# Causal masks of an attention kernel: from TensorE mask matmuls to VectorE, on one Trainium2 core

## Chip, cores and metric

The kernel runs on one core of a Trainium2 chip (trn2). The metric is the device time of one launch in microseconds (us). TensorE is called PE below, its weight loads PEld, VectorE DVE, ScalarE ACT, GpSimd POOL, and the DMA-issuing SyncE SP.

## What is computed

The input is x of shape (4, 1024, 256), 16 heads of size 64. Cut to what matters here:

```
q, k, v = x @ Wq, x @ Wk, x @ Wv                      # per head, (1024, 64)
scores  = where(causal, q @ k.T / 8, -inf)            # 1024 x 1024, lower triangle
attn    = softmax(scores)
y       = x + concat(attn @ v) @ Wo ; layernorm, gamma, beta
x       = layernorm(x + y)
x       = layernorm(x + (silu(x @ wg.T) * (x @ wu.T)) @ wd.T)
```

The softmax subtracts each row's maximum, so each score is needed twice: once for the maximum over its row, and once, with the maximum subtracted, for the exponential.

## The kernel before

The work is 4 batches times 4 groups of four heads ("quads"), so 16 iterations; each has 4 heads x 9 = 36 steps, 576 steps in all (`g`), at an average of about 2.4 us. Every engine has its own program, a loop over `g` (lines 763, 900 and the like) whose order was written out by hand; semaphores join them.

Only blocks of the lower triangle are computed. For the exponentials, scores lie with keys on the partitions and queries along the free axis, in 9 banks of 512 columns per head (`PIECES`, line 36 on); five of the nine, `k` = 0, 2, 5, 7, 8 (`DIAG`), hold one or two 128 x 128 blocks that the diagonal crosses. For the maxima, scores are computed a second time, in one pass and with queries on the partitions, in 9 banks per head (`MAXB`), 13 steps ahead (`MAX_LEAD`); five of these hold diagonal blocks (`MDIAG`): banks 0, 2, 3, 4, 6. Since 13 = 9 + 4, a step with a `DIAG` bank always carries an `MDIAG` bank, so of nine steps five have both masks and four have none.

One step `g` on PE (`step`, line 727): `scores(g)` (line 623; K1 with Q1 then K2 with Q2, two matmuls a piece, L637), in one step of nine a transpose of the maxima (L621), `max_bank` (L607), then the masks: `scores_mask(g)` (L645) and `max_mask` (L614). Each is a bf16 matmul of an identity with a 128- or 256-column mask tile that adds -1e30 in PSUM. Then `pv(g-2)` (L664), the probabilities times V in three terms. After that come "fillers" in fixed steps of the iteration: projections (L531), V (L556), the output projection (`wo_unit`, L592), and, from iteration 5 on, the feed-forward tail (`t_transpose` L687, `t_up` L710, `t_down` L722). Steps 7 to 9 and 22 to 31 of an iteration have few or no fillers.

The others, in step `g`:

- ACT: copies out of finished banks, then `exp(g)` (line 809): waits for `st_mm` (the scores bank with its mask), L813 writes the probabilities in fp32, L816 writes them again, rounded (`probs_hi`, semaphore `hi_done`).
- POOL: `probs_lo(g)` (L1114), the difference of the two; PE's `pv(g)` waits for it (`lo_done`). POOL also does the norm of the heads (L1120), the low part of the feed-forward (`t_hl`, L1156) and small statistics.
- DVE: `step` (line 1031 on): `t_y2` (L1031), `y_add` (L992), `max_row8` (L979), `max_bank` (line 951; L965 one maximum per piece; L960 both halves of bank 2 in one instruction), then the low parts of projections and V of the step before (L927, L931, L938), `recip`, low parts of raw inputs (L949), and the tail's statistics and GLU (`t_ln1`, `t_ln2`, `t_x1lo`, `t_glu` L1022 to L1025).

The buffers between them: two banks for scores (`scores(g)` waits for `hi_done` of step g-2), two for the maxima (`max_bank` waits for `mx_read` of two events before), three slots of probabilities.

```
    PIECES = [ [(0, 0, 512)], [(0, 512, 512)], [(1, 128, 384), (3, 384, 128)], ... ]
    DIAG  = {0: (0,), 2: (0, 3), 5: (0, 2), 7: (0,), 8: (0, 3)}
    MAXB  = [ [(0, 0, 128), (2, 0, 384)], [(4, 0, 512)], [(1, 0, 256), (5, 512, 256)],
              [(4, 512, 128), (6, 512, 384)], [(3, 0, 512)], [(5, 0, 512)], [(7, 512, 512)], ... ]
    MDIAG = {0: (0, 3), 2: (1, 3), 3: (0, 3), 4: (3,), 6: (3,)}
```

Of the kernel before, what the change touches and what calls it, by code (L numbers as in the profile page):

```python
# [61 lines left out]
PAIRED = 2  # L62
MDIAG = {0: (0, 3), 2: (1, 3), 3: (0, 3), 4: (3,), 6: (3,)}
# [41 lines left out]
def build(nc, xT, x, wqkv, wo, wg, wu, wd, gamma, beta, out, yscr, rscr, wscr):  # L105
    ctx = ExitStack()
    with ctx:
        def sb(name, shape, dt=F32):
            return ctx.enter_context(nc.sbuf_tensor(name, shape, dt))

        def sem(name):
            return ctx.enter_context(nc.semaphore(name))
# [32 lines left out]
        identf, identb = sb("ident_f", [P, P]), sb("ident_b", [P, P], BF16)  # L145
        maskS = sb("mask_keys_free", [P, 2, P], BF16)
        maskT = sb("mask_queries_free", [P, 2, P], BF16)
        mraw = th[:, :, :].rearrange("p a b -> p (a b)")
# [55 lines left out]
        const_step, const_b = sem("const_step"), sem("const_bf16")  # L204
# [6 lines left out]
        mx_mm, mx_read, mx_comb = sem("max_scores"), sem("max_read"), sem("max_combined")  # L211
        st_mm, exp_done, hi_done, lo_done = sem("scores_mm"), sem("exp_done"), sem("probs_hi_done"), sem("probs_lo_done")
# [20 lines left out]
        def raw_job(it, p):  # L233

            if it < NQ:
                return 4 * it + p
            return 4 * NQ + p if it == NQ else 4 * NQ + 9 + 4 * (it // NQ - 1) + p

# [257 lines left out]
        def _(pe):  # L496
# [99 lines left out]
            def max_bank(h, k):  # L596
                e, n = mx_event(h, k), h % QH
                if e >= 2:
                    pe.wait_ge(mx_read, e - 1)
                if e == 0:  # L600
                    pe.wait_ge(const_b, 1)
                if k == 0 and n % 2 == 0:
                    pe.wait_ge(proj_lo, 2 * proj_unit(h // QH, n // 2, 3) + 2)
                    pe.wait_ge(q_dup[n // 2], 32 * (h // QH + 1))
                bk, at = mxb[e % 2], 0
                for j, k0, cols in MAXB[k]:
                    last = mm(bk[:, at:at + cols], Q1[:, n, P * j:P * j + P], K1[:, n, k0:k0 + cols],  # L607
                              start=(at == 0), stop=(k not in MDIAG))
                    at += cols
                if k not in MDIAG:  # L610
                    last.then_inc(mx_mm, 1)

            def max_mask(h, k):
                mm(blocks(mxb[mx_event(h, k) % 2], MDIAG[k]), identb[:, :], maskS[:, 0:len(MDIAG[k]), :],  # L614
                   start=False, stop=True).then_inc(mx_mm, 1)
# [7 lines left out]
            def scores(g):  # L623
                h, k = divmod(g, NS)
                n = h % QH
                if g >= 2:
                    pe.wait_ge(hi_done, g - 1)
                if h < QH and k == 0:
                    pe.wait_ge(rows_set, 5)
                if k == 0:  # L630
                    pe.wait_ge(max_row[n], 16 * (h // QH + 1))
                    pe.wait_ge(k_dup[n // 2], 32 * (h // QH + 1))
                bk = stb[g % 2]
                for KX, QX in ((K1, Q1), (K2, Q2)):
                    at = 0
                    for i, q0, cols in PIECES[k]:
                        last = mm(bk[:, at:at + cols], KX[:, n, P * i:P * i + P], QX[:, n, q0:q0 + cols],  # L637
                                  start=(KX is K1 and at == 0), stop=(KX is K2 and k not in DIAG))
                        at += cols
                if k not in DIAG:  # L640
                    last.then_inc(st_mm, 1)

            def scores_mask(g):
                k = g % NS
                mm(blocks(stb[g % 2], DIAG[k]), identb[:, :], maskT[:, 0:len(DIAG[k]), :], start=False, stop=True).then_inc(st_mm, 1)  # L645
# [81 lines left out]
            def step(g):  # L727
# [8 lines left out]

# [37 lines left out]
        def _(act):  # L774
# [120 lines left out]
            act.wait_ge(const_step, 9)  # L895
            for a in range(2):
                A(maskT[:, a, :], mraw[:, 0:P], ACT.Copy)
                A(maskS[:, a, :], mraw[:, P:2 * P], ACT.Copy)
            A(identb[:, :], identf[:, :], ACT.Copy).then_inc(const_b, 1)
# [15 lines left out]
        def _(dve):  # L915
# [35 lines left out]
            def max_bank(h, k):  # L951
                e = mx_event(h, k)
                dve.wait_ge(mx_mm, e + 1)
                if k == 0 and h:
# [83 lines left out]
            def step(g):  # L1038
# [65 lines left out]
        def _(pool):  # L1104
# [53 lines left out]
            def step(g):  # L1158
# [23 lines left out]
                if 0 <= g < NG:  # L1182
# [3 lines left out]
            G.memset(mraw[:, 0:2 * P], 0.0).then_inc(const_step, 1)  # L1186
# [4 lines left out]
            pool.wait_ge(const_step, 6)  # L1191
            G.affine_select(out=identf[:, :], in_=identf[:, :], compare_op=ALU.not_equal, fill=1.0, base=0,
                            pattern=[[-1, P]], channel_multiplier=1).then_inc(const_step, 1)
            G.affine_select(out=mraw[:, 0:P], in_=mraw[:, 0:P], compare_op=ALU.is_ge, fill=MASKED, base=0,
                            pattern=[[1, P]], channel_multiplier=-1).then_inc(const_step, 1)
            G.affine_select(out=mraw[:, P:2 * P], in_=mraw[:, P:2 * P], compare_op=ALU.is_ge, fill=MASKED, base=0,
                            pattern=[[-1, P]], channel_multiplier=1).then_inc(const_step, 1)
            pool.wait_ge(const_step, 9)
# [70 lines left out]
```

## Time and profile before

| | |
|---|---|
| median of 3 runs | 1543.27 us (1542.69 to 1544.79) |
| the profiled execution | 1540.12 us |
| its span | 1538.3 us, granted TensorE clock 0.985 |
| PE / PEld busy | 1467.4 us (95%) / 1256.5 us (82%) |
| DVE / ACT / POOL busy | 896.6 (58%) / 1012.9 (66%) / 1018.2 us (66%) |
| stretch of the 576 steps | 36.4 to about 1434 us; before it the first projections and maxima, behind it the last output projection and four tails |

The profile is of one execution. "Busy" is the time in which an engine has an instruction under way; a PE matmul's row overlaps the next one's, so a mean length of a PE row is longer than what the matmul adds to the time. The chain of waits goes back from the last instruction, at each step to what released it; its pieces don't overlap, and they add up to the span.

### The profile page before, as it was taken

What the parts mean: (1) busy time and instruction counts of PE and PEld (TensorE: products, weight loads), DVE (VectorE), ACT (ScalarE), POOL (GpSimd) and SP (SyncE); (2) the same over time, 40 slices, a digit from 0 to 9 for tenths busy, and PEclk for the clock granted to TensorE, in tenths of its full rate; (3) what the DMA queues carried; (4) which work ended last, traced back from release to release, by engine and by line L of the source; (5) the groups of instructions that cost most, each with busy time, mean ns of one, the idle gap of its engine ahead of it and who ended that gap; (6) DMA issues with size and microseconds to landing.
All of it is one profiled execution on the core that took longest, in us unless ns stands there. A gap on an engine that the chain in (4) does not pass through costs nothing.

```text
span 1538.3 us, 24135 instructions
## 1 busy us (share of the span) xinstructions
PE 1467.4 (95%) x8576; PEld 1256.5 (82%) x8576; DVE 896.6 (58%) x1825; ACT 1012.9 (66%) x1926; POOL 1018.2 (66%) x964
## 2 busy tenths in 40 slices
PE   6999999999999999999999999999999999999746
PEld 5888888888888888888888888888888888888536
DVE  7555555655565655756555565665556565564256
ACT  5876767776776766767576676766667676676332
POOL 3766666666675757757576675767757576687664
PEclk9999999999999999999999999999999999999869
DMA  4232131313421221322132121222233112221000
GB/s 147 87 87 94 39 101 49 111 50 118 138 84 49 57 69 52 109 62 90 42 99 75 56 90 49 71 82 56 83 110 90 50 43 70 56 63 54 23 1 28
DMA packets 61479, 110.88 MB, mean 72 GB/s; under 512 B 16432, under 2 KB 41776, under 8 KB 61360
## 3 DMA queue, kind: packets, MB, share of 16 engines
q1 hardware_dynamic: 61360, 109.35, 24.0%
q8 instruction: 68, 1.11, 0.3%
q14 instruction: 51, 0.42, 0.1%
HBM read 61.34 MB, written 13.89 MB: 49 GB/s over the span
## 4 chain that ended last, share of the span: by engine, by line
PE 86%; POOL 6%; DVE 4%; ACT 2%; issue 1%; DMA 1%; SPq 0%; ACTq 0%; POOLq 0%; DVEq 0%
PE bank L664 24%; PE bank L637 16%; PE bank L531 11%; PE bank L607 9%; PE bank L592 8%; PE bank L556 6%; PE bank L710 5%; PE bank L722 3%; PE bank L645 2%; PE bank L614 2%; POOL probs_lo L1114 2%; POOL h_lo L1156 1%; POOL heads_T L1120 1%; DVE max_part L965 1%; DVE tanh_h L1022 1%
## 5 line engine op out<-in xcount | busy, mean ns | idle before, releaser
L1114 POOL TENSOR_TENSOR probs_lo<-probs,probs_hi 128x512 fp32r<-128x512 f32 x576 | 743.1, 1296 | 439.9 <-ACT probs_hi L816 439.0
L965 DVE TENSOR_REDUCE max_part<-bank 128x1 f32<-128x512 f32 (+2 forms) x640 | 361.6, 582 | 342.2 <-PE bank L614 217.7
L813 ACT ACTIVATE probs<-bank 128x512 f32<-128x512 f32 x576 | 344.5, 598 | 273.1 <-PE bank L645 188.7
L637 PE MATMUL bank<-Q,K 128*128 128x512 f32 (+3 forms) x1536 | 383.6, 351 | 1.5 <-ACT probs_hi L816 1.5
L816 ACT ACTIVATE probs_hi<-bank 128x512 fp32r<-128x512 f32 x576 | 341.9, 594 | 0.0
L637 PEld LDWEIGHTS bank<-Q,K 128*128 128x128 f32 x1536 | 252.4, 189 | 29.9 <-ACT probs_hi L816 2.4
L664 PE MATMUL bank<-probs_hi,VH 128*128 128x512 f32 (+3 forms) x768 | 255.3, 373 | 0.4 <-POOL probs_lo L1114 0.3
L607 PE MATMUL bank<-K,Q 128*128 128x512 f32 (+3 forms) x768 | 245.7, 361 | 2.6 <-DMA Q<-Q 2.2
L664 PE MATMUL bank<-probs_hi,VL 128*128 128x512 f32 (+3 forms) x768 | 234.6, 346 | 0.0
L664 PE MATMUL bank<-probs_lo,VH 128*128 128x512 f32 (+3 forms) x768 | 234.0, 345 | 0.0
L607 PEld LDWEIGHTS bank<-K,Q 128*128 128x128 f32 x768 | 135.3, 189 | 29.6 <-DVE max_part L965 3.2
L664 PEld LDWEIGHTS bank<-probs_hi,VH 128*128 128x128 f32 x768 | 139.5, 189 | 17.7 <-POOL probs_lo L1114 2.8
L664 PEld LDWEIGHTS bank<-probs_hi,VL 128*128 128x128 f32 x768 | 130.2, 189 | 17.0
L664 PEld LDWEIGHTS bank<-probs_lo,VH 128*128 128x128 f32 x768 | 131.3, 190 | 5.5
L592 PE MATMUL bank<-wo_quad,heads_T 128*128 128x256 f32 x512 | 124.1, 387 | 8.7 <-POOL heads_T L1120 7.4
L592 PEld LDWEIGHTS bank<-wo_quad,heads_T 128*128 128x128 f32 x512 | 95.6, 192 | 27.7 <-issue 8.9
L531 PE MATMUL bank<-xh,wh 128*128 128x512 f32 x256 | 103.7, 405 | 9.7 <-POOL wl L1202 8.6
L531 PE MATMUL bank<-xh,wl 128*128 128x512 f32 x256 | 100.9, 394 | 0.0
L531 PE MATMUL bank<-xl,wh 128*128 128x512 f32 x256 | 100.4, 392 | 0.0
L799 ACT ACTIVATE Q<-bank 64x512 fp32r<-64x512 f32 x128 | 75.6, 591 | 30.6 <-PE bank L531 28.2
L927 DVE SCALAR_TENSOR_TENSOR Q<-bank,Q 64x512 fp32r<-64x512 f32 x128 | 87.8, 686 | 5.8 <-ACT Q L799 2.8
L931 DVE TENSOR_TENSOR K<-bank,K 64x512 fp32r<-64x512 f32 x128 | 88.1, 689 | 4.9 <-ACT K L799 1.0
(139 smaller groups left out, 2287.0 us busy)
## 6 DMA issues: line engine op xcount, KB each, us to landing
Q<-Q SPq DMA_DIRECT2D x64, 256.0 KB, 3.6
K<-K SPq DMA_DIRECT2D x64, 256.0 KB, 3.4
recip_bc<-recip_scratch SPq DMA_DIRECT2D x64, 256.0 KB, 3.4
wh<-w_scratch SPq DMA_DIRECT2D x12, 768.0 KB, 4.5
wl<-w_scratch SPq DMA_DIRECT2D x12, 768.0 KB, 6.1
wo_quad<-wo SPq DMA_DIRECT2D x16, 256.0 KB, 3.0
y<-x SPq DMA_DIRECT2D x16, 256.0 KB, 3.8
x_tail<-x SPq DMA_DIRECT2D x13, 256.0 KB, 3.7
```

The costliest lines, as they stand in the source:

```text
L531: last = mm(bk[:, :], a[:, k, col:col + 2 * E], b[:, k, CH * c:CH * c + CH], start=(k == 0 and t == 0), stop=(k == KD - 1 and t == 2))
L556: last = mm(bk[:, 2 * P * t:2 * P * t + 2 * P], a[:, k, tok:tok + P], b[:, k, col:col + QH * E], start=(n == 0), stop=(n == 3 * KD - 1))
L592: last = mm(bk[:, D * t:D * t + D], HT[:, (2 * wi + r) % 3, tok:tok + P], WoS[:, r, :], start=(r == 0), stop=(r == 1))
L607: last = mm(bk[:, at:at + cols], Q1[:, n, P * j:P * j + P], K1[:, n, k0:k0 + cols], start=(at == 0), stop=(k not in MDIAG))
L637: last = mm(bk[:, at:at + cols], KX[:, n, P * i:P * i + P], QX[:, n, q0:q0 + cols], start=(KX is K1 and at == 0), stop=(KX is K2 and k not ...
L664: last = mm(pvb[c][:, b0:b0 + cols], VX[:, i, n // 2, v0:v0 + P], px[:, g % RING, at:at + cols], start=(t == 0 and k < 2), stop=(t == 2 an ...
L813: A(pe_[:, g % 2, :], stb[g % 2][:, :], ACT.Exp).then_inc(exp_done, 1)
L816: A(ph[:, g % RING, :], stb[g % 2][:, :], ACT.Exp).then_inc(hi_done, 1)
L927: V.scalar_tensor_tensor(Q2[rows, hx, cols], bk[rows, :], SCALE, Q1[rows, hx, cols].bitcast(F32), ALU.mult, ALU.subtract).then_inc(proj_lo, 1)
L931: V.tensor_tensor(K1[other, hx, cols], bk[rows, :], K1[rows, hx, cols].bitcast(F32), ALU.subtract).then_inc(proj_lo, 1)
L965: last = V.reduce_max(mp[:, j, c:c + 1], bk[:, at:at + cols], AX.X)
L1114: G.tensor_tensor(pl[:, g % RING, :], pe_[:, g % 2, :], ph[:, g % RING, :].bitcast(F32), ALU.subtract).then_inc(lo_done, 1)
```

## The change

The mask matmuls, the bf16 identity and the bf16 mask tiles go. DVE does both masks. In `max_bank`, each piece that the diagonal crosses (it ends at the diagonal block, so it is one whose `k0 + cols` is `128 j + 128`: eight per head, in banks 0, 2, 3, 4, 6) is read by one `tensor_tensor_reduce`, which adds an fp32 mask (zero but for the last 128 columns), writes the sum back over the piece in PSUM, and puts the row maximum out; bank 2 takes two such instructions instead of one reduction. A new `scores_mask(g)` on DVE adds the mask to the one or two diagonal blocks of the scores bank in place in PSUM; `exp(g)` of those banks waits for its semaphore `st_masked`. On DVE it stands in step `g` behind `t_y2` and `y_add` and in front of `max_row8` and `max_bank`. POOL builds the masks in fp32, ACT's five conversions are gone. The diff, cut to its core:

```diff
+def crossed(j, k0, cols):
+    return k0 + cols == P * j + P
...
-        identf, identb = sb("ident_f", [P, P]), sb("ident_b", [P, P], BF16)
-        maskS = sb("mask_keys_free", [P, 2, P], BF16)
-        maskT = sb("mask_queries_free", [P, 2, P], BF16)
+        identf = sb("ident_f", [P, P])
+        maskS = sb("mask_keys_free", [P, CH])
+        maskT = sb("mask_queries_free", [P, 2, P])
...
 (PE, max_bank)
-                              start=(at == 0), stop=(k not in MDIAG))
+                              start=(at == 0), stop=(at + cols == CH))
                     at += cols
-                if k not in MDIAG:
-                    last.then_inc(mx_mm, 1)
-
-            def max_mask(h, k):
-                mm(blocks(mxb[mx_event(h, k) % 2], MDIAG[k]), identb[:, :], maskS[:, 0:len(MDIAG[k]), :],
-                   start=False, stop=True).then_inc(mx_mm, 1)
+                last.then_inc(mx_mm, 1)
...
 (PE, scores)
-                if k not in DIAG:
-                    last.then_inc(st_mm, 1)
-
-            def scores_mask(g):
-                k = g % NS
-                mm(blocks(stb[g % 2], DIAG[k]), identb[:, :], maskT[:, 0:len(DIAG[k]), :], start=False, stop=True).then_inc(st_mm, 1)
+                last.then_inc(st_mm, 1)
...
 (PE, step)
-                if 0 <= g < NG and g % NS in DIAG:
-                    scores_mask(g)
-                if 0 <= h < NH and k in MDIAG:
-                    max_mask(h, k)
...
 (ACT, exp)
-                act.wait_ge(st_mm, g + 1)
+                if g % NS in DIAG:
+                    act.wait_ge(st_masked, masked_before(g) + 1)
+                else:
+                    act.wait_ge(st_mm, g + 1)
...
 (DVE, max_bank)
-                if k == PAIRED:
-                    both = mp[:, :, :].rearrange("p j c -> p (j c)")[:, 2:16:9]
-                    V.reduce_max(both, bk[:, :].rearrange("p (a b) -> p a b", a=2), AX.X).then_inc(mx_read, 1)
-                else:
-                    at = 0
-                    for j, k0, cols in MAXB[k]:
-                        c = k0 // CH
-                        last = V.reduce_max(mp[:, j, c:c + 1], bk[:, at:at + cols], AX.X)
-                        at += cols
-                    last.then_inc(mx_read, 1)
+                at = 0
+                for j, k0, cols in MAXB[k]:
+                    c, part = k0 // CH, bk[:, at:at + cols]
+                    if crossed(j, k0, cols):
+                        last = V.tensor_tensor_reduce(part, part, maskS[:, CH - cols:CH], 1.0, LOWEST, ALU.add, ALU.max, mp[:, j, c:c + 1])
+                    else:
+                        last = V.reduce_max(mp[:, j, c:c + 1], part, AX.X)
+                    at += cols
+                last.then_inc(mx_read, 1)
...
+            def scores_mask(g):
+                dve.wait_ge(st_mm, g + 1)
+                which = DIAG[g % NS]
+                part = blocks(stb[g % 2], which)
+                V.tensor_tensor(part, part, maskT[:, 0:len(which), :], ALU.add).then_inc(st_masked, 1)
...
 (DVE, step)
                         y_add(wo_due(g - 1, u), u)
+                if 0 <= g < NG and g % NS in DIAG:
+                    scores_mask(g)
                 h, rest = divmod(g + T_LEAD, NS)
                 if rest == 0 and 0 <= h < NH:
                     max_row8(h)
```

## Rows read from the trace of the kernel before

**Rows 1.** The page, busy times, and the chain of waits by engine and line
```profile
PE 1467.4 (95%) x8576; PEld 1256.5 (82%) x8576; DVE 896.6 (58%) x1825; ACT 1012.9 (66%) x1926; POOL 1018.2 (66%) x964
...
PE 86%; POOL 6%; DVE 4%; ACT 2%; issue 1%; DMA 1%; SPq 0%; ACTq 0%; POOLq 0%; DVEq 0%
```

**Rows 2.** Chain of waits, 37 to 1434 us, by line
```profile
by line: PE bank L664 26.6%; PE bank L637 17.8%; PE bank L531 11.9%; PE bank L607 9.5%; PE bank L592 7.7%; PE bank L556 6.2%; PE bank L710 4.5%; PE bank L722 2.7%; PE bank L645 2.1%; PE bank L614 1.8%; POOL probs_lo L1114 1.7%; POOL h_lo L1
```

**Rows 3.** Same chain, masked steps, then one unmasked: start us, us, what
```profile
327.96 0.13 PE bank L645
328.09 0.11 PE bank L614
...
329.60 0.07 PE bank L645
329.67 0.06 PE bank L614
329.73 0.76 PE bank L664 x3
...
333.77 0.45 PE bank L637 x2
...
334.45 0.68 PE bank L664 x3
```

**Rows 4.** Timeline, masked step without fillers: scores to pv (start us, us)
```profile
331.81 0.74 PE L637 MATMUL bank<-Q,K 128*128 128x384 f32 x4
...
333.06 0.60 ACT L813 ACTIVATE probs<-bank 128x512 f32<-128x512 f32 x1 [0.45 <-PE bank L645]
...
334.22 2.55 POOL L1114 TENSOR_TENSOR probs_lo<-probs,probs_hi 128x512 fp32r<-128x512 f32 x2 [0.74 <-ACT probs_hi L816]
...
335.64 0.42 PE L664 MATMUL bank<-probs_hi,VH 128*128 128x384 f32 x2
```

**Rows 5.** Timeline, masked step beside a projection: probs_lo to pv
```profile
705.62 1.30 POOL L1114 TENSOR_TENSOR probs_lo<-probs,probs_hi 128x512 fp32r<-128x512 f32 x1
...
708.38 0.40 PE L664 MATMUL bank<-probs_hi,VH 128*128 128x384 f32 x2
```

**Rows 6.** Groups of DVE by line and shape: busy us, mean ns, idle before
```profile
L965 DVE TENSOR_REDUCE max_part<-bank 128x1 f32<-128x512 f32 x384 | 264.9, 690 | 247.0 <-PE bank L614 123.1 <-PE bank L607 121.5
L938 DVE TENSOR_TENSOR VL<-bank,VH 128x256 fp32r<-128x256 f32 x128 | 47.8, 415 | 0.0
L992 DVE TENSOR_TENSOR y<-bank,y 128x512 f32<-128x512 f32 x64 | 44.3, 692 | 79.4 <-PE bank L592 79.4
L960 DVE TENSOR_REDUCE max_part<-bank 128x2 f32<-128x512 f32 x64 | 43.9, 686 | 43.5 <-PE bank L614 43.4
L949 DVE TENSOR_TENSOR xl<-raw,xh 128x512 fp32r<-128x512 f32 x12 | 11.0, 917 | 0.0
L972 DVE TENSOR_REDUCE max_rows<-max_part 128x8 f32<-128x16 f32 x64 | 10.9, 170 | 2.2
L1001 DVE MEMSET carrier<- 1x1 f32 x48 | 2.8, 59 | 0.0
```

**Rows 7.** Timeline, steps 25 to 27 of an iteration with a tail
```profile
772.33 0.68 DVE L1025 TENSOR_TENSOR tanh_h<-bank,tanh_h 128x512 f32<-128x512 f32 x1
...
773.09 1.29 POOL L1156 TENSOR_TENSOR h_lo<-tanh_h,h_hi 128x512 fp32r<-128x512 f32 x1 [0.53 <-DVE tanh_h L1025]
...
774.34 2.54 POOL L1114 TENSOR_TENSOR probs_lo<-probs,probs_hi 128x512 fp32r<-128x512 f32 x2
...
774.44 0.39 PE L722 MATMUL bank<-w_down,h_hi 128*128 128x256 f32 x1
...
776.29 0.48 PE L664 MATMUL bank<-probs_hi,VH 128*128 128x512 f32 x1
```

**Rows 8.** Who waited for whom: us in total, times, longest
```profile
PEld bank L592 <- DVE tanh_h L1025: 6.0, 11, 0.5
```

**Rows 9.** Chain of waits, 1408 to 1436 us, by line
```profile
by line: POOL probs_lo L1114 45.2%; POOL h_lo L1156 13.3%; POOL heads_T L1120 9.0%; PE bank L710 7.0%; ACT probs L813 6.4%; ACT probs_hi L816 5.3%; PE bank L722 4.3%; POOL rstd L1133 2.5%; ACT tanh_h L847 2.1%; PE bank L637 1.9%; issue 1.8%
```

More of the change, by code:

```diff
@@ L61 @@
 ]
-PAIRED = 2
-MDIAG = {0: (0, 3), 2: (1, 3), 3: (0, 3), 4: (3,), 6: (3,)}
+def crossed(j, k0, cols):
+    return k0 + cols == P * j + P
 MAX_LEAD = 13
@@ L143, in build @@
         carrier = sb("carrier", [1, 1])
-        identf, identb = sb("ident_f", [P, P]), sb("ident_b", [P, P], BF16)
-        maskS = sb("mask_keys_free", [P, 2, P], BF16)
-        maskT = sb("mask_queries_free", [P, 2, P], BF16)
-        mraw = th[:, :, :].rearrange("p a b -> p (a b)")
+        identf = sb("ident_f", [P, P])
+        maskS = sb("mask_keys_free", [P, CH])
+        maskT = sb("mask_queries_free", [P, 2, P])
         bank = [ctx.enter_context(nc.psum_tensor(f"bank{i}", [P, CH], F32)) for i in range(8)]
@@ L202, in build @@
         out_stored, consts_loaded = sem("out_stored"), sem("consts_loaded")
-        const_step, const_b = sem("const_step"), sem("const_bf16")
+        const_step = sem("const_step")
         zeros, rows_set = [sem("rows_cleared0"), sem("rows_cleared1")], sem("rows_set")
@@ L211, in build @@
         mx_mm, mx_read, mx_comb = sem("max_scores"), sem("max_read"), sem("max_combined")
+        st_masked = sem("scores_masked")
         st_mm, exp_done, hi_done, lo_done = sem("scores_mm"), sem("exp_done"), sem("probs_hi_done"), sem("probs_lo_done")
@@ L237, in raw_job, with masked_before @@
             return 4 * NQ + p if it == NQ else 4 * NQ + 9 + 4 * (it // NQ - 1) + p
+        def masked_before(g):
+            return len(DIAG) * (g // NS) + sum(k < g % NS for k in DIAG)
         def hi_before(it):
@@ L599, in max_bank @@
                     pe.wait_ge(mx_read, e - 1)
-                if e == 0:
-                    pe.wait_ge(const_b, 1)
                 if k == 0 and n % 2 == 0:
@@ L637, in scores @@
                         last = mm(bk[:, at:at + cols], KX[:, n, P * i:P * i + P], QX[:, n, q0:q0 + cols],
-                                  start=(KX is K1 and at == 0), stop=(KX is K2 and k not in DIAG))
+                                  start=(KX is K1 and at == 0), stop=(KX is K2 and at + cols == CH))
                         at += cols
-                if k not in DIAG:
-                    last.then_inc(st_mm, 1)
-            def scores_mask(g):
-                k = g % NS
-                mm(blocks(stb[g % 2], DIAG[k]), identb[:, :], maskT[:, 0:len(DIAG[k]), :], start=False, stop=True).then_inc(st_mm, 1)
+                last.then_inc(st_mm, 1)
             def pv(g):
@@ L894, in _ @@
                 stage_w(p + 1)
[L895 to L899, printed above, removed]
             for g in range(FIRST, END):
@@ L953, in max_bank @@
                 dve.wait_ge(mx_mm, e + 1)
+                if e == 0:
+                    dve.wait_ge(const_step, 11)
                 if k == 0 and h:
@@ L1185, in _ @@
             G.memset(identf[:, :], 0.0).then_inc(const_step, 1)
-            G.memset(mraw[:, 0:2 * P], 0.0).then_inc(const_step, 1)
+            G.memset(maskT[:, :, :], 0.0).then_inc(const_step, 1)
+            G.memset(maskS[:, :], 0.0).then_inc(const_step, 1)
             G.memset(halves[:, :], -0.5).then_inc(const_step, 1)
@@ L1190, in _ @@
             G.memset(eps_ln[:, :], LN_EPS).then_inc(const_step, 1)
-            pool.wait_ge(const_step, 6)
+            pool.wait_ge(const_step, 7)
             G.affine_select(out=identf[:, :], in_=identf[:, :], compare_op=ALU.not_equal, fill=1.0, base=0,
                             pattern=[[-1, P]], channel_multiplier=1).then_inc(const_step, 1)
-            G.affine_select(out=mraw[:, 0:P], in_=mraw[:, 0:P], compare_op=ALU.is_ge, fill=MASKED, base=0,
-                            pattern=[[1, P]], channel_multiplier=-1).then_inc(const_step, 1)
-            G.affine_select(out=mraw[:, P:2 * P], in_=mraw[:, P:2 * P], compare_op=ALU.is_ge, fill=MASKED, base=0,
+            for a in range(2):
+                G.affine_select(out=maskT[:, a, :], in_=maskT[:, a, :], compare_op=ALU.is_ge, fill=MASKED, base=0,
+                                pattern=[[1, P]], channel_multiplier=-1).then_inc(const_step, 1)
+            G.affine_select(out=maskS[:, CH - P:CH], in_=maskS[:, CH - P:CH], compare_op=ALU.is_ge, fill=MASKED, base=0,
                             pattern=[[-1, P]], channel_multiplier=1).then_inc(const_step, 1)
-            pool.wait_ge(const_step, 9)
+            pool.wait_ge(const_step, 11)
             for p in range(4):
```

## Prediction

> **What bounds the kernel now.** I read the page's busy times and chain first [rows 1]: PE is busy 95% of the span and is 86% of the chain, DVE is busy 58% and is 4% of it. Narrowed to the 576 steps [rows 2], the chain is PE almost throughout; the two mask lines L645 and L614 are 2.1% and 1.8% of those 1397 us. So the mask matmuls lie on the path. Piece by piece [rows 3], a step with 256-column masks has 0.13 + 0.11 us for them, one with 128-column masks 0.07 + 0.06. Behind the latter the three matmuls of `pv` take 0.76 us, where the same group behind an unmasked maximum bank takes 0.68: the reader is to see that a short mask matmul also leaves the next weight load partly uncovered. The unmasked step runs from 333.77 to 335.13, 1.36 us.
>
> Then the slack of what is handed from engine to engine. In a masked step without fillers [rows 4], scores start at 331.81 and exp 1.25 us later; POOL starts the first of two `probs_lo` at 334.22, 0.08 us after ACT is done, and each takes about 1.29 us, so it ends at 335.51; PE's `pv` for it starts at 335.64. Slack: 0.13 us. Beside a projection [rows 5] it is 708.38 - 706.92 = 1.46 us. Counted over the 320 masked steps, 28 have under 0.5 us (the first, with 0.18, has its scores at 36.4 us, the last, with 0.05, at 1432.0); 24 of them lie in iterations 0 to 4 and 4 in the last. Their mean is 0.27. From iteration 5 to 14 the tails' fillers leave no masked step under 0.5.
>
> **What is removed from PE.** The chain's 3.9% of 1397 us is 54.5 us. The uncovered load comes on top: 0.76 - 0.68 = 0.08 us at most, and I take 0.06 us, in the two of nine steps whose last mask has 128 columns, 128 times in all: 7 us. Gross 61 us. PE's queue loses 640 matmuls. No DMA is added or moved, and SP's program is the same. ACT loses five conversions in front of the first step, and POOL gains two small instructions there; both wait for the first loads at that time, and with that cover gone it would be under 1 us.
>
> **What is added on DVE.** No row shows the new operations, so bounds from [rows 6]:
>
> - The add in place in the scores bank, 192 times 256 columns and 128 times 128. A tensor_tensor that reads PSUM takes 415 ns at 256 columns (L938) and 692 at 512 (L992), 1.08 ns a column, so 276 at 128. Nothing is the lower end, 0.69 us the upper; I take 0.415 and 0.28: 80 + 36 = 115 us of DVE. It writes PSUM, which no row of DVE shows.
> - The masked maximum, 512 times. The plain one is 690 ns at 512 columns, the tensor_tensor 692: the same within 2 ns, so the lower end is no extra, and I take it. The upper end is a second pass, about 1.04 ns a column.
> - Putting the maximum out may be an instruction of its own: between nothing and the 170 ns of L972, with L1001's 59 ns as the smallest row. I take 70 ns: 512 x 0.07 = 36 us.
> - Bank 2 in two parts: 2 x 0.415 - 0.686 = 0.14 us, 64 times: 9 us.
>
> The trace can't tell whether that 70 ns is there. The Trainium skill, "VectorE: DVE Perf Modes", section "Two Vector instructions with no wait between them", says that an operation that also writes out its accumulator is two instructions. By it the 36 us of DVE stand, without it they fall; no row of this profile shows which.
>
> DVE then has 897 + 115 + 36 + 9 = 1057 us, some 71% of the new span: by its sum it is not the bound. DVE's new operations take one operand from SBUF and one from PSUM, as L992 does at 692 ns; only L949 with two SBUF operands is lengthened (917), so I leave POOL's and DVE's other durations as they are.
>
> **What moves in the hand-offs.** Exp of a masked bank now waits for DVE instead of the mask matmul behind the maximum bank. Before, it starts 1.25 us into the step [rows 4]. Now scores end at 0.74, and DVE needs 0.09 + 0.415 + 0.09 us, with the gap between engines as above: 1.33. That is 0.08 later with DVE free, and DVE is free in the steps without fillers, where it has the maxima alone. The path to `pv` gets 0.08 longer while PE's two steps get shorter by up to 0.24 + 0.18 us, so about 0.5 us of slack is used up. In the 28 steps with less, the rest is a new stall: 28 x (0.5 - 0.27) = 6 us. What is late next there is POOL's `probs_lo`, released by ACT's second exp.
>
> Where DVE is busy with other work, the mask queues behind it, and the maxima behind the mask. The longest such wait is in step 25 of an iteration with a tail [rows 7]: GLU holds DVE until 773.01, so the mask ends near 773.4, the exps near 774.65. POOL is held by `h_lo` until 774.38 anyway, so `probs_lo` starts near 774.7 instead of 774.34 and ends at 776.0, just in front of `pv` at 776.29, which itself comes some 0.2 earlier. It is hidden with nothing to spare: each 0.1 us more on DVE costs 0.1 us there.
>
> **Where the saving is lost.** In those steps PE meets a chain that no mask is in: GLU on DVE, `h_lo` on POOL until 774.38, then `t_down` at 774.44 [rows 7]. The masks of steps 25 and 26 (0.18 + 0.24 us) only lengthen PE's wait. Likewise step 11, where `wo_unit` already waits for DVE's GLU [rows 8]: 0.18. So 0.6 us in each of 10 iterations: 6 us. In the last 28 us of the steps POOL is the chain [rows 9]: masks save little there, and two later exps cost about 0.4 us each: 1 us. In front of the first step DVE's maxima are on the path, and some eight longer ones cost 1 us.
>
> **The sum.** 54.5 + 7 - 6 - 6 - 1 - 1 = 47.5 us. The profiled execution took 1540.1 us (span 1538.3), so 1492.6; the median of the runs stands 3.15 us above it, so I predict 1496 us. With neither stalls nor lost savings it is 61 us, i.e. 1482; with the add at 0.69 us and 170 ns for each read-out, some 0.3 us more in about 60 steps, near 1514.
>
> **Rivals.**
>
> - Half-rate masked maximum. 2560 masked columns a head x 1.04 ns is 2.7 us a head, 170 us in all: DVE at 1227 us, 81%. Masks then stand behind maxima that are 0.53 us longer at 512 columns, and the step of rows 7 and its like stall: 0.5 us in three steps of each iteration returns 25 us: 1521. For it: two streams and a maximum put out in one instruction. Against: tensor_tensor and reduction cost the same here [rows 6]. In the Trainium skill, "Vector Engine (DVE) Microarchitecture Reference", section "Points that are easy to get wrong", one such form runs at half throughput with two non-bf16 sources in SBUF. Here one source is in PSUM, so by the letter it keeps full rate; read widely, it gives this rival's 1521. Chance 0.12.
> - ACT and POOL become the round. POOL needs 1.29 + 0.08 us a step, PE's unmasked step takes 1.36 [rows 3, 4]. If a stall doesn't stay in its step but holds up the following ones, the filler-free third gives all its savings back, about 20 us: 1516. Against: after a stall PE is late and the next step has its slack again. Chance 0.08.
> - Slower: the hand-off through DVE is long. Place: each masked step, between scores and exp. If the add in place cost 1.9 us instead of 0.42, all steps under about 2 us of slack would stall; at 0.23 us on average over the 320, since most have 0.5 us and more to take it up, it returns 74 us: 1570. It decides from 0.15 us a masked step (47.5 / 320), which by the slacks needs an add of about 1.4 us. For it: a write to PSUM by DVE isn't in the trace, and DVE is in order. Against: its PSUM reads of 256 and 512 columns have no such fixed part. Chance 0.10.
> - The masks' PE time was only cover: PE would wait for something else anyway, and time stays at 1543. Against: rows 2 put it on the chain. Chance 0.04.
>
> **How the numbers follow.** The forecast has the rest, 0.66. A measurement of this kernel can tell about 0.2% (3 us) from no change. Faster: 0.66 + 0.12 + 0.08 = 0.86; same 0.04; slower 0.10. The range holds the forecast with its bounds and the two rivals that end near 1520: 1483 to 1524.
>
> **What would show it.** Right: no L645 or L614 rows; masked steps shorter on PE by 0.13 to 0.24 us; mask adds near 415 and 280 ns; DVE near 1057 us; exp's idle time ended by DVE; small new PE waits for `probs_lo`, and waits for `h_lo` longer by 0.4 us each. Wrong: masked maxima near 1.2 us at 512 columns (first rival); PE waits of tens of us for `probs_lo` or `probs_hi` (second or third); a PE chain not shortened (fourth).

## The result: faster, by 35 us instead of 47

The changed kernel takes 1508.14 us (median of 4 runs, 1506.43 to 1508.49), the kernel before 1542.98 us on the same chip. The ratio is 0.9774, with a 95% interval of 0.9757 to 0.9791. The direction was as forecast, the time lies inside the range, and 12 us of the forecast gain are missing. The profiled execution took 1508.49 us, with a span of 1506.7 us. Against the span before of 1538.3 that is 31.6 us, and the accounts below are made between such spans: against them the sum of 47.5 is 15.9 us too high.

Busy times and the chain by engine, as in [rows 1]:

```profile
PE 1413.7 (94%) x7936; PEld 1226.0 (81%) x7936; DVE 1008.4 (67%) x2721; ACT 1001.6 (66%) x1921; POOL 1020.9 (68%) x966
...
PE 77%; DVE 10%; POOL 8%; ACT 3%; issue 2%; DMA 0%; ACTq 0%; SPq 0%; POOLq 0%; DVEq 0%
```

The 640 mask matmuls are gone and PE is busy 53.7 us less. In the chain DVE has gone from 4% to 10% and PE from 86% to 77%: some of what PE gave up now belongs to other engines.

DVE's groups by line and shape, answering to [rows 6]:

```profile
L954 DVE TENSOR_REDUCE max_part<-bank 128x1 f32<-128x512 f32 x256 | 176.5, 690 | 103.9 <-PE bank L612 101.7
L952 DVE CUSTOM_DVE_ANT_0 bank<-bank,mask_keys_free 128x512 f32<-128x512 f32 x128 | 88.5, 692 | 0.5 <-PE bank L612 0.4
...
L968 DVE TENSOR_TENSOR bank<-bank,mask_queries_free 128x256 f32<-128x256 f32 x192 | 82.7, 431 | 85.1 <-PE bank L637 84.2
L952 DVE CUSTOM_DVE_ANT_0 bank<-bank,mask_keys_free 128x384 f32<-128x384 f32 x128 | 76.5, 597 | 0.0
L952 DVE DVE_READ_ACCUMULATOR2_ANT max_part<- 128x1 f32 x512 | 71.5, 140 | 0.3
...
L968 DVE TENSOR_TENSOR bank<-bank,mask_queries_free 128x128 f32<-128x128 f32 x128 | 37.3, 291 | 64.0 <-PE bank L637 63.8
```

L952 is the masked maximum: 692 ns at 512 columns against 690 for the plain one (L954). L968 is the mask of the scores, 431 and 291 ns in place in PSUM, where 415 and 280 were taken. Each masked maximum is followed by a row of its own that puts the accumulator out, 512 of them at 140 ns.

Who waited for whom (line that waited, what released it, us in total, times, longest), PE's weight loads in the kernel after; of before, L722 and L607 had 23.4 and 3.2 us, and L592 is in [rows 8]:

```profile
PEld bank L717 <- POOL h_lo L1154: 30.2, 25, 3.5
...
PEld bank L612 <- DVE max_part L952: 16.1, 34, 0.9
...
PEld bank L599 <- DVE tanh_h L1021: 8.5, 11, 0.8
...
PEld bank L659 <- POOL probs_lo L1112: 8.0, 17, 1.1
PEld bank L637 <- ACT probs_hi L809: 5.8, 5, 2.7
```

The first and third are longer by 6.8 and 2.5 us, where the masks' time only lengthens a wait, as forecast; with no mask at all (`no_masks`, below) they are 30.0 and 8.5 us. The second, 3.2 us before, was not in the prediction: the maxima's bank (`max_bank`, L612) waits for DVE to have read the bank before. The fourth is the hand-off through `probs_lo` that the prediction priced.

### Where the time is, stretch by stretch

The steps can be compared by the start of their first scores matmul in the trace. The spans of the profiled executions, in us (three of the columns are experiments, described below):

| stretch | before | no_masks | plain_max | after | mixed |
|---|---|---|---|---|---|
| up to step 0 | 36.4 | 38.1 | 36.3 | 38.2 | 37.9 |
| iteration 0 | 67.2 | 63.8 | 69.0 | 69.3 | 65.9 |
| iterations 1 to 4 | 326.3 | 311.5 | 313.9 | 315.1 | 312.1 |
| iterations 5 to 14 | 920.7 | 887.4 | 892.9 | 897.1 | 891.2 |
| iteration 15, to its last step | 82.7 | 80.2 | 82.4 | 82.2 | 80.6 |
| from there to the end | 105.1 | 104.7 | 106.3 | 104.7 | 106.5 |

The last stretch differs by 2 us and more between profiles of the same kernel (104.7 and 108.1 us in two of `after`), and in several profiles one single step of the 576 is about 1 us longer than its like in the other iterations, each time another one (before: step 26 of iteration 4; after: step 8 of iteration 10). Differences of about 1 us between single rows of this table are therefore not evidence. The forecast was for gains everywhere; iteration 0 is 2.1 us slower than before.

### The profile page after: what moved, and what is told of

Read it like the earlier page. It is cut to its first block, busy times and chain, and to the rows that moved or that the text cites. A ratio compares the mean times of both kernels' runs of the same rounds, so it can differ in the third digit from the quotient of the medians.

```text
span 1506.7 us, 23750 instructions
## 1 busy us (share of the span) xinstructions
PE 1413.7 (94%) x7936; PEld 1226.0 (81%) x7936; DVE 1008.4 (67%) x2721; ACT 1001.6 (66%) x1921; POOL 1020.9 (68%) x966
## 4 chain that ended last, share of the span: by engine, by line
PE 77%; DVE 10%; POOL 8%; ACT 3%; issue 2%; DMA 0%; ACTq 0%; SPq 0%; POOLq 0%; DVEq 0%
PE bank L659 21%; PE bank L637 15%; PE bank L538 12%; PE bank L612 8%; PE bank L599 8%; PE bank L563 5%; PE bank L705 5%; PE bank L717 3%; POOL h_lo L1154 2%; POOL probs_lo L1112 2%; DVE max_part L954 2%; POOL heads_T L1118 1%; DVE h_hi L1020 1%; DVE tanh_h L1021 1%; DVE tanh_h L1018 1%
## 5 line engine op out<-in xcount | busy, mean ns | idle before, releaser
L612 PE MATMUL bank<-K,Q 128*128 128x512 f32 (+3 forms) x768 | 247.0, 363 | 8.1 <-DVE max_part L952 5.8
L954 DVE TENSOR_REDUCE max_part<-bank 128x1 f32<-128x512 f32 x256 | 176.5, 690 | 103.9 <-PE bank L612 101.7
L952 DVE CUSTOM_DVE_ANT_0 bank<-bank,mask_keys_free 128x128 f32<-128x128 f32 (+3 forms) x512 | 243.7, 507 | 2.6 <-PE bank L612 2.3
L659 PE MATMUL bank<-probs_hi,VH 128*128 128x512 f32 (+3 forms) x768 | 231.5, 342 | 3.6 <-POOL probs_lo L1112 3.1
L968 DVE TENSOR_TENSOR bank<-bank,mask_queries_free 128x256 f32<-128x256 f32 (+1 forms) x320 | 120.0, 375 | 149.2 <-PE bank L637 148.0
L612 PEld LDWEIGHTS bank<-K,Q 128*128 128x128 f32 x768 | 135.8, 190 | 39.6 <-DVE max_part L952 16.1
```

Source lines behind the costliest of these rows:

```text
L659: last = mm(pvb[c][:, b0:b0 + cols], VX[:, i, n // 2, v0:v0 + P], px[:, g % RING, at:at + cols], start=(t == 0 and k < 2), stop=(t == 2 an ...
L952: last = V.tensor_tensor_reduce(part, part, maskS[:, CH - cols:CH], 1.0, LOWEST, ALU.add, ALU.max, mp[:, j, c:c + 1])
L954: last = V.reduce_max(mp[:, j, c:c + 1], part, AX.X)
L968: V.tensor_tensor(part, part, maskT[:, 0:len(which), :], ALU.add).then_inc(st_masked, 1)
```

## Experiments

In the expectations, theory A is that the maxima (longer on DVE, and behind the mask) are the larger part of what is missing, and theory C that the hand-off of the scores through DVE is; theory D is about the start. Diffs are against the kernel after.

### no_masks, max_on_pe, scores_on_pe: which half costs what

`no_masks` leaves both masks out, so nothing is causal; it shows what PE's saving is worth with no new work on DVE. `max_on_pe` and `scores_on_pe` put one of the two masks back as the bf16 matmul of before, behind the maxima's bank.

```diff
 (no_masks; ACT, exp)
-                if g % NS in DIAG:
-                    act.wait_ge(st_masked, masked_before(g) + 1)
-                else:
-                    act.wait_ge(st_mm, g + 1)
+                act.wait_ge(st_mm, g + 1)
 (no_masks; DVE, max_bank: plain reduce_max for every piece, bank 2 in one; DVE, step)
-                if 0 <= g < NG and g % NS in DIAG:
-                    scores_mask(g)
```

```diff
 (max_on_pe; PE, step; maxima plain on DVE)
+                if 0 <= h < NH and max_on_pe(h, k):
+                    max_mask(h, k)
```

```diff
 (scores_on_pe; PE, step; no mask add on DVE, exp waits for st_mm)
+                if 0 <= g < NG and g % NS in DIAG:
+                    scores_mask(g)
```

> Leaves out both masks on every engine (no causal mask; plain maxima, no add), the rest as in the changed kernel. Theory A (the saving of PE time is all there, some 1.0 to 1.1 us a head, and the missing 12 us of my sum went into waits behind the new DVE work): 1480 to 1488 us, and PE waits for DVE's maxima at the k = 6 steps back to about 3 us. Rival B (removing the matmuls gives PE less than I summed): about 1500 or more, little better than the changed kernel's 1508.

Measured: 1487.53 us (1486.65 to 1488.95), ratio 0.9652 [0.9635, 0.9669]. PE's saving alone is worth 52.8 us, and DVE's new work gives 20.6 us of it back (21.0 between the spans; the kernel before took 1542.98 us beside the one median and 1540.31 beside the other, so the 20.6 is good to some 3 us).

> Maxima masked by PE matmuls as before the change, scores masked by DVE as after it. Theory A: half of the PE time comes back (+34 us against no masks at all) but the waits for DVE's maxima behind the transpose (16 us of weight-load waits) go: 1512 to 1518 us. If the hand-off through exp were the costly part (rival C) its stalls stay and it is 1522 or more.

Measured: 1531.56 us (1526.66 to 1533.55), ratio 0.9932 [0.9907, 0.9957].

> Scores masked by PE matmuls as before, maxima masked by DVE as after. Theory A: the waits behind the masked maxima at the k = 6 steps stay in part (bank 0 is 0.28 us + 0.25 us longer, but no add stands in front of it): 1518 to 1524 us. Rival C (hand-off through exp is the costly part): as low as 1512.

Measured: 1526.93 us (1526.1 to 1527.52), ratio 0.9905 [0.9886, 0.9925].

The first is what theory C expected, the second lies above the expectations of both theories. Each half alone gains far less than half: 8.8 and 13.4 us, together 22 where the whole gives 34 to 35. The steps show one reason. A step with k = 0 takes 1.559 us with both mask matmuls, 1.503 with either and 1.360 with none: the pair costs 0.20 us, one alone already 0.14 of it (k = 5: 1.716, 1.589, 1.474). So halves cannot be added up for these kernels; they don't settle which part of DVE's work costs the 20.6 us. That needed the next group.

### plain_max and no_scores_mask: one half of DVE's work without a matmul in its place

`plain_max` leaves the mask out of the maxima, so that they also cover the masked keys of the diagonal blocks; the scores are masked as in the kernel after. The softmax then subtracts a number that can be larger than the row's maximum, which drops out in the division but for underflow. `no_scores_mask` leaves out the mask of the scores and keeps the masked maxima.

```diff
 (plain_max; DVE, max_bank; bank 2 in one reduction)
-                    if crossed(j, k0, cols):
+                    if False:
```

```diff
 (no_scores_mask; DVE, step; exp waits for st_mm)
-                if 0 <= g < NG and g % NS in DIAG:
-                    scores_mask(g)
```

> The changed kernel with plain maxima: the maximum over a diagonal block takes in the keys that the mask would have left out (the softmax subtracts a number that can be larger than the row's maximum), scores masked by DVE. Theory A (the waits behind the masked maxima are the larger part of what DVE's new work costs): 1490 to 1496 us, against 1487.5 with no masks and 1508 with both. Rival C (the hand-off of the scores through DVE is the larger part): 1499 or more. Beside the run with the maxima masked by PE (1531.6) it also gives what one mask matmul a step costs PE.

Measured: 1502.06 us (1501.11 to 1502.62), ratio 0.9739 [0.9721, 0.9756].

> The changed kernel without the mask of the scores (the exponentials take in the keys behind the diagonal inside the diagonal blocks), maxima masked by DVE. Theory A: the masked maxima are the larger part, so 1496 to 1502 us; the wait in step 6 of iterations 5 to 14 is about 0.5 us instead of 0.9. Rival C: 1492 or less.

Measured: 1489.67 us (1488.79 to 1490.78), ratio 0.9661 [0.9646, 0.9675].

Over `no_masks`, the masks of the scores alone cost 1502.06 - 1487.53 = 14.5 us, the masked maxima alone 2.1 us, and both together 20.6. Some 4 us seem to come only when both are there, though that is hardly more than such medians can tell. The steps show it in one place: step 15 of iterations 5 to 14 takes 3.036 us with no masks or with masked maxima alone, 3.05 with plain maxima and 3.167 with both. Theory A falls: the masks of the scores on DVE are the larger part. That is not yet the hand-off to exp alone, since such a mask also delays what stands behind it on DVE; the next experiment is on that.

### swap_k5: the maxima in front of the mask, where the next bank waits

In a step with k = 6 PE transposes the row maxima, and that transpose takes one of the two banks of the maxima. So `max_bank` of that step reuses the bank that DVE reads in the step before, where k = 5 and a mask stands in front. The timeline of the kernel after, steps 5 and 6 of an iteration with a tail (start us, us, what, idle before with its releaser):

```profile
705.94 0.43 DVE L968 TENSOR_TENSOR bank<-bank,mask_queries_free 128x256 f32<-128x256 f32 x1
...
706.28 0.29 DVE L952 CUSTOM_DVE_ANT_0 bank<-bank,mask_keys_free 128x128 f32<-128x128 f32 x1
706.42 0.27 PE L621 MATMUL bank<-ident_f,max_rows 128*8 128x128 f32 x1
...
706.49 0.60 DVE L952 CUSTOM_DVE_ANT_0 bank<-bank,mask_keys_free 128x384 f32<-128x384 f32 x1
...
707.00 0.14 DVE L952 DVE_READ_ACCUMULATOR2_ANT max_part<- 128x1 f32 x1
...
707.20 0.50 PE L612 MATMUL bank<-K,Q 128*128 128x512 f32 x1 [0.51 <-DVE max_part L952]
```

and the same bank in the kernel before:

```profile
720.87 0.76 DVE L965 TENSOR_REDUCE max_part<-bank 128x1 f32<-128x128 f32 x2
...
721.59 0.27 PE L621 MATMUL bank<-ident_f,max_rows 128*8 128x128 f32 x1
721.67 0.19 PEld L607 LDWEIGHTS bank<-K,Q 128*128 128x128 f32 x1 [0.23 <-DVE max_part L965]
721.67 0.50 PE L607 MATMUL bank<-K,Q 128*128 128x512 f32 x1
```

Before, DVE's two maxima end at 721.63 and the matmul follows at 721.67; only the weight load in front of it waited, 0.23 us. After, DVE starts them 0.34 us behind its mask and needs 0.86 us with the read-outs (706.28 to 707.14) instead of 0.76, and PE stands idle for 0.51 us. `swap_k5` puts the maxima first in the steps whose successor does this transpose and had the wait (5 and 14 of the iteration).

```diff
+                late = s in (5, 14)
-                if 0 <= g < NG and g % NS in DIAG:
+                if 0 <= g < NG and g % NS in DIAG and not late:
                     scores_mask(g)
...
                     max_bank(h, k)
+                if 0 <= g < NG and g % NS in DIAG and late:
+                    scores_mask(g)
```

> The changed kernel, but in steps 5 and 14 of an iteration DVE does the masked maxima of bank 0 in front of the scores mask. Theory A (PE's max bank of the next step waits for the read of bank 0, since the transpose takes the other bank): the wait in step 6 of iterations 5 to 14 (0.9 us in the trace) falls by the 0.43 us of the add, that of step 15 (0.13 us) goes: 1500 to 1504 us. Rival: the wait there ends by something else, 1508 and unchanged step 6.

Measured: 1506.80 us (1505.46 to 1508.01), ratio 0.9776 [0.9758, 0.9794].

`swap_again` is the same kernel, and `after_again` the kernel after, both once more on one chip.

> The changed kernel again, on the chip of the next run: 1508 us, within 2 us.

Measured: 1506.89 us (1505.96 to 1510.48), ratio 0.9776 [0.9758, 0.9795].

> The kernel with DVE's maxima of bank 0 in front of the scores mask in steps 5 and 14 again, beside the changed kernel. Summed by steps its trace has 0.4 us less in each of iterations 5 to 14 and 1.4 us more in iteration 0, so 2 to 4 us below the changed kernel; no difference if the step sums don't carry over to the whole.

Measured: 1506.68 us (1505.44 to 1507.97), ratio 0.9771 [0.9755, 0.9786].

No gain can be measured, against the 4 to 8 and the 2 to 4 us expected, though step 6 of the tail iterations goes from 3.699 to 3.366 us (before: 3.011) and step 15 from 3.167 to 3.036. In the profiles, iterations 5 to 14 are 4.7 us shorter in `swap_again` than in the kernel after, but iteration 0 is 1.8 us longer (71.1 against 69.3; 71.5 in `swap_k5`). Iteration 15 is 0.9 us longer in `swap_again` and 0.4 shorter in `swap_k5`, and the end 1.1 and 2.1 us longer, which is the spread of these stretches. The wait is real and step 6 shortens by 0.33 us when it is relieved; part of that is given back in iteration 0. The same reordering makes exp later there, but that this is the reason was not tried by itself.

### start_on_pe: the first steps and the clock

In front of the first steps DVE has the low parts of K and Q to make, and a mask of the scores now queues behind them. The chain of the kernel after, 36 to 50 us (start us, us, what):

```profile
39.67 0.69 DVE K L919
...
40.39 0.69 DVE K L919
...
41.11 0.31 DVE bank L968
...
41.45 0.60 ACT probs L806
42.04 0.50 ACT probs_hi L809
...
42.58 1.33 PE bank L637 x4
```

The scores of step 2 wait for `probs_hi` of step 0, since there are two banks, so PE stands still. The busy time of each engine in stretches of 2 us (stretch, length, PE, PEld, DVE, ACT, POOL busy with their counts, granted TensorE clock as a share of 2.4 GHz, DMA share, GB/s), in the kernel after:

```profile
40.00:42.00 2.00, 0.19 (x1) 0.00 (x0) 1.94 (x6) 0.56 (x2) 0.00 (x0) 0.96 0.78 172
42.00:44.00 2.00, 1.42 (x5) 1.36 (x5) 0.66 (x4) 1.51 (x4) 1.32 (x2) 0.50 0.26 90
44.00:46.00 2.00, 2.00 (x6) 1.55 (x6) 1.14 (x3) 1.08 (x2) 1.54 (x2) 0.50 0.00 0
46.00:48.00 2.00, 2.00 (x6) 1.60 (x5) 0.69 (x1) 1.08 (x2) 1.08 (x2) 0.50 0.00 0
48.00:50.00 2.00, 2.00 (x11) 1.73 (x10) 0.71 (x2) 0.92 (x2) 1.12 (x1) 0.83 0.00 0
```

PE was busy 0.19 us between 40 and 42 us, and behind that the granted clock is 0.50, its 1.2 GHz level, up to 48 us, where PE is full and does 6 matmuls in 2 us. Step 1 takes 3.715 us instead of 1.358. The Trainium skill, "TensorE: Matmul & The Clock Gate", section "What's actually happening", says that the clock has two states and which one holds depends on how busy PE has been of late; these rows agree.

`start_on_pe` masks the scores of steps 0 and 2 on PE, right behind the scores; the bf16 operands are the high halves of the fp32 tiles.

```diff
+        def scores_on_pe(g):
+            return g in (0, 2)
...
 (PE, scores)
+                if scores_on_pe(g):
+                    if g == 0:
+                        pe.wait_ge(const_step, 11)
+                    last = mm(blocks(bk, DIAG[k]), high16(identf[:, :]), high16(maskT[:, :, :].rearrange("p a b -> p (a b)")[:, 0:P * len(DIAG[k])]),
+                              start=False, stop=True)
                 last.then_inc(st_mm, 1)
...
 (ACT, exp; and the same condition in front of scores_mask on DVE)
-                if g % NS in DIAG:
+                if g % NS in DIAG and not scores_on_pe(g):
```

> The changed kernel with the scores masks of steps 0 and 2 alone done by a PE matmul right behind the scores. Theory D (in the first steps the mask queues behind DVE's low parts of K, PE stands idle for over 1 us, and its granted clock falls to 0.50 for some 6 us): PE is not idle from 40 to 42 us, the granted clock stays at 1.00 there, and the time is 3 to 5 us below the changed kernel: 1502 to 1505 us. Rival (the stall only moves to the next wait, or the low clock there has another cause): 1507 to 1508.

Measured: 1505.11 us (1502.79 to 1506.16), ratio 0.9763 [0.9748, 0.9777]. Its same stretches:

```profile
40.00:42.00 2.00, 1.45 (x8) 1.13 (x9) 1.93 (x5) 1.52 (x4) 2.00 (x2) 1.00 0.94 240
42.00:44.00 2.00, 2.00 (x11) 1.65 (x10) 1.35 (x3) 1.30 (x3) 1.77 (x2) 1.00 0.00 0
44.00:46.00 2.00, 2.00 (x15) 1.92 (x14) 0.91 (x3) 1.27 (x3) 1.67 (x2) 1.00 0.00 0
46.00:48.00 2.00, 2.00 (x10) 1.55 (x10) 1.66 (x7) 1.52 (x4) 1.27 (x2) 1.00 0.00 0
```

The clock stays at its full level, step 1 takes 1.457 us, and iteration 0 takes 65.2 us instead of 69.3. That settles the start in the profile: two masks behind DVE's queue cost 4.1 us, the low clock included. The maxima have no large part in it: with plain ones (`plain_max`) PE stands still just as long, 0.00 us busy from 38 to 40 us, and the clock falls to 0.50, while without the masks of the scores (`no_scores_mask`) step 1 takes 1.579 us. Between the medians only 1.8 us are seen, within the spread of the runs, so the gain of the whole is not shown (1505.11 is at the upper edge of the 1502 to 1505 expected); in this profile iteration 15 and the end are 3.0 us longer than in the kernel after.

### mixed and mixed_plain: each mask where there is room for it

`mixed` keeps DVE's masks wherever the hand-off has slack, and puts the scores mask on PE in 38 of the 320 masked steps: in iteration 0 steps 0, 2, 8, 11, 14, 23, 26, 29; in 1 to 4 steps 8, 23, 26, 29; in 5 to 14 step 5; in the last 5, 23, 26, 29. In step 14, where DVE masks, the maxima go first. `mixed_plain` has the plain maxima of `plain_max` besides.

```diff
+        def scores_on_pe(g):
+            it, s = divmod(g, NST)
+            if it == 0:
+                return s in (0, 2, 8, 11, 14, 23, 26, 29)
+            if it <= NQ:
+                return s in (8, 23, 26, 29)
+            return s in ((5,) if it < NIT - 1 else (5, 23, 26, 29))
...
 (DVE, step)
+                on_dve = 0 <= g < NG and g % NS in DIAG and not scores_on_pe(g)
+                if on_dve and s != 14:
                     scores_mask(g)
...
+                if on_dve and s == 14:
+                    scores_mask(g)
```

> Scores masks on PE, right behind the scores, in those steps only where the hand-off showed a stall (steps 0, 2, 8, 11, 14, 23, 26, 29 of iteration 0; 8, 23, 26, 29 of iterations 1 to 4; 5 of iterations 5 to 14; 5, 23, 26, 29 of the last), and the maxima in front of the mask in step 14. By the step sums: 3 to 4 us at the start, 0.45 x 4 in iterations 1 to 4, 0.4 x 10 in 5 to 14, 1.2 in the last: 1496 to 1500 us. If a mask matmul costs more there than the 0.12 to 0.16 us that it costs alone in a step, 1502 or more.

Measured: 1496.18 us (1495.15 to 1497.19), ratio 0.9707 [0.9692, 0.9721]. It beats both kernels: 10.7 us under `after_again` (on another chip; the kernel before took 1541.5 us on the one and 1541.9 on the other), with 38 mask matmuls more.

> The same with plain maxima (the maximum over a diagonal block takes in the keys that the mask would have left out): what is left of the hand-off alone. 1491 to 1495 us, against 1502 for plain maxima with all scores masks on DVE and 1487.5 with no masks; above 1497 the stalls don't come from the steps chosen.

Measured: 1494.61 us (1492.19 to 1497.2), ratio 0.9694 [0.9677, 0.9711]. That is 1.6 us under `mixed`, with the ranges overlapping: once the tight steps are relieved, the masked maxima cost next to nothing.

How a tight hand-off looks on either side. Steps 29 to 31 of an iteration without a tail, kernel after:

```profile
329.20 0.74 PE L637 MATMUL bank<-Q,K 128*128 128x384 f32 x4
...
329.98 0.43 DVE L968 TENSOR_TENSOR bank<-bank,mask_queries_free 128x256 f32<-128x256 f32 x1 [0.68 <-PE bank L637]
...
330.51 0.60 ACT L806 ACTIVATE probs<-bank 128x512 f32<-128x512 f32 x1 [0.51 <-DVE bank L968]
...
331.67 2.54 POOL L1112 TENSOR_TENSOR probs_lo<-probs,probs_hi 128x512 fp32r<-128x512 f32 x2 [0.55 <-ACT probs_hi L809]
...
333.02 0.51 PE L659 MATMUL bank<-probs_hi,VH 128*128 128x384 f32 x2
```

and in `mixed`, where step 29 is masked on PE (L655):

```profile
323.30 0.74 PE L649 MATMUL bank<-Q,K 128*128 128x384 f32 x4
...
323.87 0.29 PE L655 MATMUL bank<-mask_queries_free,ident_f 128*128 128x256 bf16 x1
...
324.26 0.60 ACT L823 ACTIVATE probs<-bank 128x512 f32<-128x512 f32 x1 [0.17 <-PE bank L655]
...
325.43 2.65 POOL L1132 TENSOR_TENSOR probs_lo<-probs,probs_hi 128x512 fp32r<-128x512 f32 x2 [0.27 <-ACT probs_hi L826]
...
326.96 0.40 PE L676 MATMUL bank<-probs_hi,VH 128*128 128x384 f32 x2
```

Exp starts 1.31 us into the step with DVE's mask and 0.96 us with the mask right behind the scores. The 0.35 us reach POOL, and `pv` starts 3.82 us after the scores in the one, 3.66 in the other; step 31 takes 1.777 against 1.496 us. PE pays 0.06 us for the mask in step 29 (1.571 to 1.630) and gets 0.28 back two steps later. The waits of PE's weight loads in `mixed` show the same over the kernel:

```profile
PEld bank L734 <- POOL h_lo L1174: 30.1, 25, 3.5
...
PEld bank L624 <- DVE max_part L969: 8.1, 19, 0.8
...
PEld bank L676 <- POOL probs_lo L1132: 3.5, 9, 0.7
```

The waits for the maxima and for `probs_lo` are halved (16.1 and 8.0 before the edit); the wait for `h_lo`, in which no mask takes part, stays. By the table above `mixed` gains 3.4 us in iteration 0, 3.0 in 1 to 4, 5.9 in 5 to 14 and 1.6 in 15. Not every one of the 38 masks pays: in iterations 1 to 4, steps 8 to 10 together take 4.96 to 5.10 us with the mask of step 8 on PE, and 4.95 to 5.10 with it on DVE.

## Why the prediction was right, and where it fell short

**What bounds.** Right. PE is the path, and taking the masks from it is worth most of its 54.5 us.

**Saving on PE, gross 61, less 6 where PE waits for `h_lo` and GLU: 55.** Right in size: `no_masks` measures 52.8 us. A step with k = 0 loses 0.20 us and one with k = 5 0.24, where 0.19 and 0.24 were counted. Where the saving was to be lost, it is lost. Step 25 of a tail iteration goes from 1.588 to 1.416 us and step 26 from 3.007 to 3.173, so together they gain nothing; step 11 stays at 3.70. That DVE's mask in step 25 would be hidden is right too: step 26 takes 3.171 us with it and 3.173 without. Of the 2 us that are missing, 1.7 are not the masks' time: PE's clock is 0.50 already at 22 to 24 us in `no_masks` and `after`, behind a gap at 18 to 20 in which PE is busy 0.01 us (0.80 before), and step 0 starts 1.7 to 1.8 us later. Why that gap appears with some versions and not with `plain_max`, which starts at 36.3 us, was not tried. A further 0.24 us a tail iteration is lost in step 6, even without masks 3.246 us against 3.011. That is just what step 5 gained (1.716 to 1.474 us): PE waits for the maxima's bank there too, 6.5 us in all in `no_masks` against 3.2 before. It is a third place where the saving only lengthens a wait, and the prediction didn't have it. The two make 4 us lost that were not counted, against 2 to 3 us missing, so the 55 is also right because errors partly cancel.

**The operations on DVE.** Right, and cheap: 431 and 291 ns for the mask, 692 for the masked maximum, so no half rate. The accumulator is put out by an instruction of its own, as the page "VectorE: DVE Perf Modes" of the Trainium skill has it ("Two Vector instructions with no wait between them"). Its row is 140 ns, twice what I took, but on DVE it adds less: in the timeline above the maximum of 384 columns starts at 706.49 with a row of 0.60, and its accumulator read starts at 707.00, inside that row. Back to back, the next instruction starts 0.616 us after a masked maximum of 512 columns and 0.608 after a plain one, 0.515 against 0.464 at 384 columns, and 0.341 after a mask of 256 columns whose row is 0.431. DVE's rows thus overlap by 0.08 to 0.09 us, and its busy time rose by 112 us, to 1008, where adding up rows gave 160 and 1057. For whoever waits for the maximum, the read is not hidden: it ends at 707.14, and PE goes on at 707.20.

**The hand-off through DVE: 28 steps, 6 us.** This is the step that failed. Where I had counted it, it fits: exp was to start 1.33 us into the step and starts at 1.31, step 31 lost 0.26 us against before, and iterations 1 to 4 with the last one lose 3.6 + 2.0 = 5.6 us to DVE's work (after less `no_masks`). The closeness of 5.6 to 6 is in part luck: 8 of the 28 steps lie in iteration 0, and the steps in which such a stall lands, 25, 28 and 31, make 2.1 us in iterations 1 to 4 and 1.4 in the last. What failed is what was drawn from the sentence "From iteration 5 to 14 the tails' fillers leave no masked step under 0.5". As a count it holds (the least slack there is 0.60 us), but I had looked at one hand-off only, from the scores to `pv`. In those iterations the kernel after is 9.7 us slower than `no_masks`: 0.45 us in step 6, 0.15 in step 29, 0.13 in step 15 of each, together 7.4; of the rest 1.1 us are the one long step 8 of iteration 10 and 0.7 are in step 3. For step 6 the cause is shown: PE waits for the bank of the maxima, whose reading now stands behind the mask. The longer maxima alone add 0.11 there (`no_scores_mask`, 3.360), the mask alone 0.33 (`plain_max`, 3.580). For step 29, which takes 3.453 us in `no_scores_mask` as in `no_masks`, and 3.606 in `plain_max` and in `mixed`, the scores masks are the cause, but which of them was not tried.

**In front of the first steps, 1 us.** It failed as well. Up to step 0 the longer maxima cost nothing that can be seen (38.2 us against 38.1 in `no_masks`), while iteration 0 loses 5.5 us to DVE's work, 4.3 of them in its first five steps. Steps 0 and 2 were among the 28, at 0.3 us each; that the mask of step 0 queues behind K's low parts was not counted, nor that PE's standstill of 2 us is followed by some 6 us at the low clock.

**In the last 28 us, 1 us.** Iteration 15 as a whole loses 2.0 us, mainly in steps 25, 28 and 31 (3.106 to 3.572, 3.313 to 3.833, 3.172 to 3.623), with 0.45 in step 6, and it sits inside the 5.6 above. In the three steps it is the same hand-off, with POOL as the path [rows 9], at 0.45 to 0.52 us each where 0.4 was said.

So DVE's work was priced at 6 + 1 + 1 = 8 us and costs 21.0 between the spans: 9.7 in iterations 5 to 14 (nothing forecast) and 5.5 in iteration 0, with 5.6 in the others. Of the 15.9 us that the sum is too high between the spans, 13.0 are this difference and 2.9 the saving (54.5 + 7 - 6 = 55.5 against 52.6). The range of 1483 to 1524 was wide enough to hold it.

**Rivals.** Half rate: no, 692 ns. ACT and POOL as the round: no. Iterations 1 to 4 keep 11.2 of the 14.8 us that `no_masks` gains there. The hand-off through DVE as a loss on the whole: its mechanism is at work, and it is the larger part of what is missing, but at 14.5 us over 320 steps it is 0.05 us a step where 0.15 were needed, and the add takes 0.43 us, not 1.4. Masks as mere cover: no.

## What to carry to other kernels

Before moving work onto an engine that "has time", list every consumer of that engine and find for each what it holds up: here also the double-buffered bank that only one step in nine makes tight. Check the first steps by themselves, since a single wait there can also cost clock. And a move need not be all or nothing: 38 of 320 masks left on the busy engine brought back some 11 us of the 20 that DVE's work cost.

## Unexpected of the hardware

- Of two short bf16 mask matmuls in a step, the first costs 0.14 us and the second 0.06 (step k = 0: 1.360, 1.503, 1.559 us). Where it stands can count too: in step 8 of iterations 1 to 4 one scores mask costs 0.14 us behind the maxima's bank (`scores_on_pe`, 1.699) and 0.08 right behind the scores (`mixed`, 1.636), over 1.561 with none. In step 23 the place makes no difference (1.632 and 1.635, over 1.507). The operands differ as well, bf16 tiles in the one and high halves of fp32 tiles in the other, so the cause is open.
- A standstill of PE of about 2 us was followed by some 6 us at half the clock: 0.19 us busy between 40 and 42 us, then 0.50 from 42 to 48. With 1.45 us busy in the same stretch, the clock stayed at 1.00.
- The accumulator's read has a row of 140 ns, but in 292 of the 512 cases another DVE instruction starts within 3 ns of it. Back to back, a DVE row of 0.690 us is followed by the next start after 0.608.
